# Streaming 17 columns in place of 102 in the products of the attention weights with the values

## What is computed

```python
q = proj(layernorm(x), w_q, b_q); k = proj(ctx, w_k, b_k); v = proj(ctx, w_v, b_v)
scores = einsum('bhqd,bhkd->bhqk', q, k) / sqrt(16)          # causal mask
out = einsum('bhqk,bhkd->bhqd', softmax(scores), v)          # the products with the values
x = x + tanh(g_xattn) * (out @ w_o.T + b_o)
x = x + tanh(g_ffn) * experts(layernorm(x))                  # 8 experts, top 2, exact gelu
```

## Time and profile before

| | |
|---|---|
| three runs | 912.01, 915.75 and 917.88 us, median 915.75 us |
| the profiled execution | 919.0 us, its span 917.2 us |
| mean granted TensorE clock over the span | 0.953 |
| busy over the span | PE 823.5 us, PEld 747.4 us, DVE 601.8 us, ACT 439.6 us, POOL 342.1 us |
| attention stage | from the start to about 434 us |
| experts | from about 458 us to the end |

### The profile page before, as it was taken

One profiled execution on the slowest core, in us unless ns is written; L12 is line 12 of the kernel. 1 busy time (PEld: TensorE's weight loads), 2 busy tenths in 40 slices (PEclk: granted clock), 3 DMA queues, 4 the chain that ended last, 5 costly groups with the idle time before them and its releaser, 6 DMA issues. The chain is left out here.

```text
span 917.2 us, 24759 instructions
## 1 busy us (share of the span) xinstructions
PE 823.5 (90%) x7472; PEld 747.4 (81%) x7473; DVE 601.8 (66%) x1492; ACT 439.6 (48%) x962; POOL 342.1 (37%) x365
## 2 busy tenths in 40 slices
PE   4599899999999999998178999999999999999990
PEld 3489898989899889887167989999899899898880
DVE  2358889999899988887554555555555555555550
ACT  2156456656656545555044444445544544444540
POOL 2233455555555445554302332222332233232232
PEclk9699999999999999998579999999999999999995
DMA  9766888777868887882587323323323222322222
GB/s 184 152 125 133 153 174 173 153 148 152 170 171 201 202 206 203 199 186 83 204 286 251 53 49 51 52 49 51 59 50 54 50 49 49 53 49 39 25 25 26
DMA packets 87947, 108.80 MB, mean 119 GB/s; under 512 B 12832, under 2 KB 81568, under 8 KB 85664
## 3 DMA queue, kind: packets, MB, share of 16 engines
q1 hardware_dynamic: 72448, 87.17, 40.6%
q0 software_dynamic: 14304, 19.15, 13.2%
q10 hardware_dynamic: 1088, 1.11, 0.4%
HBM read 46.82 MB, written 34.36 MB: 89 GB/s over the span
## 5 line engine op out<-in xcount | busy, mean ns | idle before, releaser
L1234 POOL DMA_INDIRECT out_rows<-yg,xs x78 | 128.2, 1643 | 329.8 <-ACT yg L1276 197.9
L1366 PE MATMUL bank<-xh,wts 128*128 128x256 f16 x1872 | 212.8, 274 | 0.0
L1382 PE MATMUL bank<-wts,hh 128*128 x1872 | 210.6, 273 | 0.0
L1366 PEld LDWEIGHTS bank<-xh,wts 128*128 x1872 | 184.1, 98 | 22.0 <-issue 0.2
L1382 PEld LDWEIGHTS bank<-wts,hh 128*128 128x128 f16 x1872 | 183.2, 98 | 21.2
L1266 ACT ACTIVATE hf<-bank,b1t,gscale 128x256 f32<-128x256 f32 x312 | 154.8, 562 | 22.9 <-PE bank L1366 22.7
L510 POOL TENSOR_SCALAR_AFFINE_SELECT xs<-rowmax 128x512 bf16<-128x512 bf16 x128 | 93.7, 732 | 161.7 <-DVE rowmax L754 146.0
L1005 PE MATMUL bank<-va,probs 128*128 128x102 f32 x1024 | 139.8, 278 | 7.1 <-DVE ao L703 6.7
L1005 PEld LDWEIGHTS bank<-va,probs 128*128 128x128 f32 x1024 | 126.7, 193 | 10.4 <-DVE ao L703 5.1
L1276 ACT ACTIVATE yg<-yb,xs 128x256 f32<-128x256 f32 x78 | 35.4, 500 | 199.5 <-DVE yb L1315 189.2
L1305 DVE SCALAR_TENSOR_TENSOR hh<-hf,hscale,hh 128x512 f16<-128x512 f32 x156 | 117.2, 751 | 5.6
(11 more groups left out here) (165 smaller groups left out, 1063.1 us busy)
## 6 DMA issues: line engine op xcount, KB each, us to landing
wts<-in_W SPq DMA_DIRECT2D x16, 1024.0 KB, 7.4
wts<-keys SPq DMA_DIRECT2D x96, 128.0 KB
wts<-queries SPq DMA_DIRECT2D x96, 128.0 KB
xs<-token_rows SPq DMA_DIRECT2D x39, 272.0 KB, 2.8
split_weights<-wts SPq DMA_DIRECT2D x8, 1024.0 KB, 5.1
wts<-split_weights SPq DMA_DIRECT2D x8, 1024.0 KB, 7.3
xin<-in_x SPq DMA_DIRECT2D x16, 256.0 KB, 2.7
cin<-in_ctx_in SPq DMA_DIRECT2D x16, 256.0 KB, 3.6
```

The costliest lines, as they stand in the source:

```text
L1234: pool.indirect_dma_start(out=out[:, :], out_offset=bass.IndirectOffsetOnAxis(ap=numbers, axis=0), in_=yg[m % 2][:, half, :], in_offset=No ...
L1366: last = pe.matmul(HB[c // 2][:, c % 2 * TILE:(c % 2 + 1) * TILE], wts[:, bass.ds(expert[1], 1), at:at + P], xh[b][:, xp, k, :], start=q = ...
L1382: last = pe.matmul(YB[b][:, half * D:(half + 1) * D], hh[b][:, hp, c, half * P:(half + 1) * P], wts[:, bass.ds(expert[0], 1), at:at + D], ...
```

## The change

One constant changes. The access pattern of the moving operand at L1006 repeats a head's 17 columns once in place of six times, and the output slice at L1005 has 17 columns in place of 102.

```diff
@@ -22,7 +22,7 @@
 NG = B // GT
 PAIRS = HEADS // 2
 VA = DK + 1
-WIDE = 6
+WIDE = 1
 MANY = 8
```

## The result

The changed kernel takes 934.61 us (median of 4 executions, 924.26 to 942.38) against 916.82 us before; the ratio is 1.0157, with a 95% interval of 1.0114 to 1.0199. It is slower, by about 18 us from median to median, where 41 us were forecast. The profiled execution was the quickest of them: 924.26 us, its span 922.5 us, 5.3 us over that of before. A second set of executions, further down, has a median of 936.24 us.

A forecast was written before the change was run, and what follows sets the result against it. It took TensorE to bound both stages, VectorE close behind in attention. No direct gain, and two half-clock stretches per group at 1.54 us, 49 us less 8 us already there, made 41 us: from 915.75 to 957 us, range 914 to 1010.

The forecast's parts named there:

- The mechanism: Attention stage: the clock follows the time in which TensorE moves data, so thinner products make it fall; 41 us slower.
- what bounds the stage: Attention stage: TensorE first, with 0.69 us free per group of 23.85 us; VectorE close behind with 2.1 us.
- The first rival: Clock follows loads or matmuls in hand, so idle time alone; the change does nothing, 914 to 918 us; chance 0.19.
- I therefore cost the direct gain at nothing: Products with the values: the float32 weight load sets record spacing, so 1024 records come no closer; gain zero.
- Then nearly every one of the 16 groups falls: Group ends, steps 6 and 7: 1.16 us less streaming exceeds the 0.73 us that sufficed; nearly all 16 fall, not five.
- A distance to the edge: Group's end: 0.73 us later queries separated a group that kept the clock from one that fell.
- Two stretches per group: From steps 5 or 6 on, two slow stretches of 3.4 us per group: 49 us, less 8 us already there.
- The rival with one stretch per group: The clock falls once per group, the rest as before: 17 us more, 933 us; chance 0.22.
- The price of a stretch: Attention groups: each 3.4 us stretch at half clock adds 1.54 us; VectorE's slack hides none of it.
- The sum: Attention stage: 2 x 1.54 x 16 = 49 us, less 8 us already there, gives 41 us more.

The follow-up runs named there:

- A second set of executions: The changed kernel run again with no edit, beside the kernel before: 936.24 us, ratio 1.0192 (1.0135 to 1.0249).
- the execution of 928.4 us: Another profiled execution of the changed kernel, no edit: 930.16 us, span 928.4 us, mean clock 0.932, 126 us at 0.50.
- that of 928.3 us: Profiled execution of the unedited changed kernel, from its repeat with median 936.24 us: span 928.3 us, mean clock 0.937, 117 us at 0.50.

## Why the prediction was wrong, point by point

**The mechanism: right; what bounds the stage: in part.** Thinner products make the clock fall in the attention stage, the experts do not move, and the time moves with the clock. The first rival (width is nothing to the clock) fell with the kernels that stream three times and once beside the same loads. Whether it is the columns streamed that count, or the results written for them, no run separates. Nor does idle time alone tell the kernels apart: from 60 to 430 us TensorE's waits add up to 15.5 us before, to 16.3 us in the changed kernel and to 16.5 us with 119 columns, where the clock stayed at 1.00 from 109.80 to 430.60. The Trainium skill's page "TensorE: Matmul & The Clock Gate", section "Why this matters for your kernels", names idle gaps between matmul bursts; here the trace differs: the fall at 154.70 us came behind waits of 0.30 and 0.29 us. That TensorE alone sets the pace of the stage is not borne out: its products got shorter by more than the groups did, as the next point shows.

**"I therefore cost the direct gain at nothing": mis-sized.** It is small, but not nothing. A set in the flow, of the changed kernel and of the kernel before (timeline, the set and what follows it):

```profile
149.16 1.01 PE L1005 MATMUL bank<-va,probs 128*128 128x17 f32 x8
150.03 0.38 PE L912 MATMUL bank<-wts 128*128 128x128 bf16 x4
```
```profile
211.80 1.09 PE L1005 MATMUL bank<-va,probs 128*128 128x102 f32 x8
212.73 0.38 PE L912 MATMUL bank<-wts 128*128 128x128 bf16 x4
```

0.87 us against 0.93 us. The median over the 115 and 123 whole sets at full clock is 0.863 and 0.925 us, and 0.939 us with 119 columns. What is gained is 0.06 us at the start of a set: from its first record to the second it is 0.082 us with 17 columns, 0.143 us with 102 and 0.157 us with 119 (medians). Every later record, and the next instruction, follows at 0.112 us in all of them. The set that the prediction read, 207.90 to 208.77, stands behind the output product and is one of the shortest of before. Eight sets make 0.5 us per group, and the groups gain less. Those without a fall (from one L989 to the next, without the first two groups and the last one) took 24.09 us on average in 23 groups of the changed kernel (three executions), 24.41 us in 20 groups with 102 and 119 columns. But that is not like with like: groups that are among the longest before fell in all three executions of the changed kernel, and are missing from its mean. At the eight places in the order of groups that ran without a fall on both sides it is 24.06 against 24.22 us, so 0.16 us per group, some 2.4 us in 15. Some of the rest went into waits (TensorE's for `pay` from 60 to 430 us, before and in the changed kernel: us in total, times, longest):

```profile
PE bank L887 <- DVE pay L722: 1.6, 10, 0.2
```
```profile
PE bank L887 <- DVE pay L722: 3.5, 14, 0.3
```

**"Then nearly every one of the 16 groups falls": this step failed.** It held the 1.16 us of streaming that the change takes out of two sets against the 0.73 us of idle time that had gone with a fall, as if one could stand for the other in every group. But both places that it read have a wait for the queries, of 0.57 and of 1.30 us, and not every group has one. The end of a group, in a group that fell and in the next one, which did not (timeline of TensorE, changed kernel):

```profile
152.02 0.44 PE L887 MATMUL bank<-ident,pay 128*128 128x128 f32 x2 [0.30 <-DVE pay L722]
...
153.94 0.34 PE L989 MATMUL bank<-partsum,ones 128*128 128x4 f32 x2
154.57 1.77 PE L1005 MATMUL bank<-va,probs 128*128 128x17 f32 x8 [0.29 <-DVE ao L703]
156.18 0.67 PE L887 MATMUL bank<-ident,ao 128*128 128x128 f32 x2
157.42 0.60 PE L912 MATMUL bank<-wts 128*128 128x128 bf16 x4 [0.57 <-DMA wts<-queries]
...
179.31 0.44 PE L887 MATMUL bank<-ident,pay 128*128 128x128 f32 x2 [0.24 <-DVE pay L722]
...
181.22 0.34 PE L989 MATMUL bank<-partsum,ones 128*128 128x4 f32 x2
181.85 1.06 PE L1005 MATMUL bank<-va,probs 128*128 128x17 f32 x8 [0.29 <-DVE ao L703]
182.77 0.41 PE L887 MATMUL bank<-ident,ao 128*128 128x128 f32 x2
183.02 0.39 PE L912 MATMUL bank<-wts 128*128 128x128 bf16 x4
```

The same instructions, and up to the fall the same waits within 0.06 us; at 154.57 the set runs into half clock, 1.61 us to the next instruction, at 181.85 it takes 0.92 us. Behind the fall the first group's scores still wait for the queries, the second's do not. In the profiled execution 7 of 15 groups between the first and the last L989 have a fall, with 34 us at 0.50, ten stretches; in the execution of 928.4 us it is 6 falls and 44 us, thirteen stretches; before 5 and five. So 5 to 8 stretches more, where 27 were forecast.

What the groups that fell have in common is the idle time of TensorE just ahead of the next group's first scores (L912). Counted over the 15 group ends of each profiled execution:

| columns | group ends with 0.4 us or more idle there | of these with a fall | longest such wait without a fall, us |
|---|---|---|---|
| 17 (three executions) | 19 | 16 | 1.14 |
| 51 | 8 | 6 | 0.95 |
| 102 | 8 | 4 | 0.71 |
| 119 | 6 | 2 | 1.51 |

At the other group ends of these kernels none fell, 26 of them in the changed kernel. (One more fall stands inside the last group, at a wait for `ao` of 1.9 to 2.0 us, in all executions but that with 119 columns.) So with 17 columns no group end without such a wait lost the clock; the thinner products let shorter waits do. (For 51, 102 and 119 columns it is one execution each.) A wait in the timeline and then the stretch with its clock, at 17 columns (execution of 928.4 us) and at 119 columns:

```profile
155.49 0.40 PE L912 MATMUL bank<-wts 128*128 128x128 bf16 x4 [0.42 <-DMA wts<-queries]
156.20:159.50 3.30, 3.30 (x16) 2.94 (x13) 2.89 (x8) 1.19 (x3) 1.74 (x3) 0.50 0.82 293
```
```profile
353.70 0.40 PE L912 MATMUL bank<-wts 128*128 128x128 bf16 x4 [1.51 <-DMA wts<-queries]
109.80:430.60 320.80, 305.64 (x2907) 284.21 (x2906) 287.45 (x864) 186.18 (x429) 167.51 (x206) 1.00 0.78 173
```

A distance to the edge, read at two places that both have a wait, was applied to all 16 groups; before, seven of the 15 group ends have none. Streaming taken away did not stand in for it. What decides in detail stays open: at 154.70 and 304.90, and at 53.7 us in the execution of 928.4 us, the clock fell ahead of the wait, and waits of 0.68, 0.82 and 1.14 us kept it with 17 columns. No run moved a group's end in time and left its columns alone, so whether the moment counts is not tested. With the router's columns gone too, groups fall without such a wait (at 242.60 behind 0.24 and 0.29 us), and the time of that kernel, 956.60 us, is next to the 957 us that were forecast for the change. That is luck: it has some 33 more stretches than before, at 1.2 us each, not 27 at 1.54.

**"Two stretches per group": mis-sized with it.** Of the 19 falls in the attention stage of the changed kernel's three profiled executions 11 last one stretch and 6 two, and the last group's can last much longer (64.8 us from 415.6 us in one execution, its end past the stage). The rival with one stretch per group said 933 us, next to the 934.61 us measured, but not for its reason: it had 11 more falls of one stretch each.

**The price of a stretch: near for the first, too high for the second.** From L989 to L989 the changed kernel's groups took 24.09 us without a fall, 26.79 us with one stretch (9 groups) and 27.67 us with two (4 groups). The first 2.70 us hold the longer waits that often go ahead of a fall, as the 2.27 us of before did; the second stretch adds 0.88 us, not 1.54. These too are means over different groups. In the last group the forecast's price holds: it took 21.02 us with one stretch before, and 22.51, 26.59 and 26.90 us with 2, 4.6 and 4.9, about 1.5 us each. Over whole executions, 0.28 to 0.33 us per us at the lower clock is 1.0 to 1.1 us a stretch. Where the rest goes was not tried; that VectorE or the DMAs have caught up by then, and that later waits get shorter, is only argued.

**The sum.** Forecast were 27 more stretches at 1.54 us, 41 us. In the profiled execution two more groups fell than before, and three falls lasted for a second stretch, one of them in the last group: 2 x 2.70 + 2 x 0.88 + 1.5 = 8.7 us, less 2.4 us of direct gain, is 6.3 us; its attention stage from L989 to L989 is 376.80 - 372.20 = 4.6 us longer. For the execution of 928.4 us (one more fall, three further stretches and 3.9 in the last group) the same sum gives 8.8 us and the rows 7.6 us; for that of 928.3 us (one more fall, 3.6 further stretches in the last group) it gives 5.7 us, as its rows do (377.90 us). So the terms, with the sizes that the runs showed, give the difference to within 2 us, no closer. The median execution, with a span of 932.7 us, has 134 us at 0.50 where the profiled one has 105, some 8 stretches, and is 10 us longer.

## What to carry to other kernels

Columns that a matmul streams under a weight load that is longer anyway cost next to nothing (here 0.06 us per eight records) and can hold the clock up; before they are taken out as useless, look at how often the clock already falls at that place, and behind what wait. An effect that depends on an edge is not summed over all places from one place on either side: find out which of them have what the edge depends on (here a wait) and what part crosses, and expect executions of one kernel to differ (spans of 922.5 to 934.8 us here). A wait that TensorE has anyway can be filled with matmuls whose result nobody reads, if they end before the wait does; beside wide products and a wider router the kernel was 0.5% faster for it, and with thin products no gain is shown.

## What the hardware showed that was not expected

- The same instructions behind the same waits kept the clock in one group and lost it in another (181.85 and 154.57 us), and executions of one kernel had 105 to 140 us at 0.50.
- How long a wait the clock outlasted went with the columns around it: 1.51 us with 119 columns held, 0.42 us with 17 did not, though 1.14 us did once.
- At half clock a busy TensorE did not always get the clock back: 16.31 of 16.70 us of scores, masks and thin products left it at 0.50.
- A set of eight float32 products is 0.06 us shorter with 17 columns than with 102, though its records from the second on are equally far apart; it is the first one that is followed sooner (0.082 against 0.143 us).
- Taking 0.39 us of streaming per group out of the router cost 0.3% beside wide products, and over 2% beside thin ones.
